# Group attention of a four-layer transformer kernel: first value products in halves, and the contexts and output projections of two blocks joined in one slot each

## Chip, cores and metric

One core of a Trainium2 chip runs the whole program in one launch. The metric is device time in microseconds (us), the median of several executions. All times of instructions come from one profiled execution.

## What is computed

The reference is a residual stack of four parts over x of shape (4, 1024, 256): a windowed attention, a mixture of experts, a second attention over groups, and an expert layer with sinkhorn gates. The change touches only the second attention. Cut to what matters:

```python
Q = x @ wq + bq;  K = x @ wk + bk;  V = x @ wv + bv      # x: (B, S, E) = (4, 1024, 256)
Q, K, V = (t.reshape(B * H, S, D) for t in (Q, K, V))    # H = 16, D = 16
attn = softmax(einsum('bqd,bkd->bqk', Q, K) / sqrt(D))
ctx = einsum('bqk,bkd->bqd', attn, V).reshape(B, S, E)
out = ctx @ wo + bo + x                                  # then a layer norm
```

The plain reshape makes each "head" a group of 64 consecutive tokens with its 256 columns, read as 1024 rows of 16 numbers. So there are 64 independent attentions of 1024 queries by 1024 keys.

## The kernel before

The phases run one after another, with barriers between them. `group_attention` is the phase of the change. It works in 32 **blocks** of 16 **units**. A block is two groups in two halves of the array (h) for one half of the queries; blocks 2m and 2m+1 are a **pair** and together give the tokens of one output tile pair.

TensorE (PE) walks through numbered steps s. Step s does the plain scores of unit s (L1857, two products of 48x512 into one double PSUM bank), of which VectorE (DVE) takes the row maxima (L1781). 26 steps later (LAG), with `back = s - 26`, it does the transposed scores of the same unit (L1870, two products into a ring of three banks), whose exponentials ScalarE (ACT) takes (L1812). The products L1857 and L1870 of a step use different halves of the array's rows and run side by side. Every two steps `weigh` multiplies four exponential tiles with the values (L1886) and adds into one bank, `b_o`. A block has eight such products, each split into two halves of 256 columns on an even and on the following odd step, except the first (kt = 0): it runs at its full width of 512 columns on the even step, and the odd step has none. It waits for ACT's copy of the last block's sums (`o`, L1818), since both use `b_o`.

Each block then needs four transposes of `o` on PE (`context`, L1894, at back % 16 == 6), a reciprocal and a product on DVE (L1792, L1794). Each pair needs four more transposes (`context_T`, L1901), two copies on ACT (L1824), and for each of its blocks an output projection (`project`, L1911), a sum into x and its statistics on DVE (L1800, L1802).

Scores, contexts and projections share two double banks, the **slots** `b_s`. They are used in turn in the order of `step_uses`: PE may write use n only when DVE has read use n-2 (`slot_of`). Order on every engine is that of the program text, so nothing overtakes. SP and POOL only move data: the maxima of a block become a row of the queries by DMAs (`maxima`, L1737 and L1769), which must land before the block's transposed scores, ten steps later, and SP loads the coming queries, keys and values.

Of the kernel before, what the change touches and what calls it, by code (L numbers as in the profile page):

```python
# [14 lines left out]
P = 128  # L15
# [1619 lines left out]
def group_attention(nc, g, parts, values, qs, ks, v):  # L1635
# [12 lines left out]
    MAX_IN = 16 * 2 * P // BL  # L1648
    SHARE = 5
    RB = UB // 2  # L1650
    STEPS = UNITS + LAG + UB + 14

    def block_of(b):
        return b // 4, b // 2 % 2, b % 2
# [12 lines left out]
    def step_uses(s):  # L1667

        uses = [("scores", s)] if s < UNITS else []
        b, j = (s - LAG) // UB - 1, (s - LAG) % UB  # L1670
        if 0 <= b < BLOCKS and j == 6:
            uses.append(("context", b))
        if 0 <= b < BLOCKS and b % 2:
            uses += [("project", b - 1)] * (j == 11) + [("project", b)] * (j == 13)
        return uses

    def transposed_context(back):

        return back // (2 * UB) - 1 if back > UB and back % (2 * UB) == 8 else None

    uses = [use for s in range(STEPS) for use in step_uses(s)]
    use_place = {use: n for n, use in enumerate(uses)}
# [8 lines left out]
    with phase(nc) as (e, semaphore, begin):  # L1691
# [7 lines left out]
        rsum = [sb(f"rsum{s}", [P, HQ, NG]) for s in range(2)]  # L1699
# [71 lines left out]
        @block.vector  # L1771
        def _(dve):
            dve.wait_ge(nmax_zero, ONE + 2)
            for s in range(STEPS):
                for kind, arg in step_uses(s):
                    use = use_place[kind, arg]
                    slot = b_s[use % 2]
                    dve.wait_ge(use_done, ONE + use + 1)
                    if kind == "scores":
                        at, b = column(arg), arg // UB  # L1780
                        nc.vector.tensor_reduce(nmax[b % 2][:, at:at + 1], slot[:], axis=AX.X, op=ALU.max,  # L1781
                                                negate=True).then_inc(use_read, 1)
                        if arg % UB == UB - 1:
                            if b >= 2:
                                dve.wait_ge(max_in[0][b % 2], ONE + MAX_IN * (b // 2))
                                dve.wait_ge(max_in[1][b % 2], MAX_IN * (b // 2))
                            dve.wait_ge(use_read, ONE + use + 1)
                            nc.vector.transpose(max_rows[b % 2][:].bitcast(F32), nmax[b % 2][:].bitcast(F32)).then_inc(rows_ready, 1)  # L1788
                    elif kind == "context":
                        hf = arg % 2  # L1790
                        src = slot[:, 0:HALF].rearrange("p (q n r) -> p q n r", n=NG, r=BL)
                        nc.vector.reciprocal(rsum[hf][:], src[:, :, :, DH]).then_inc(rsum_ready, 1)  # L1792
                        dve.wait_ge(rsum_ready, ONE + arg + 1)
                        nc.vector.tensor_tensor(ctxn[:, :, HQ * hf:HQ * (hf + 1)].rearrange("p n q d -> p q n d"),  # L1794
                                                src[:, :, :, 0:DH],
                                                rsum[hf][:].unsqueeze(3).broadcast_to([P, HQ, NG, DH]), ALU.mult).then_inc(use_read, 1)
                    elif kind == "project":
                        c, gp, h = block_of(arg)
                        t = 2 * (2 * c + h) + gp
                        nc.vector.tensor_tensor(g.x[:, t, :], slot[:, 0:D], g.x[:, t, :], ALU.add).then_inc(use_read, 1)  # L1800
                        dve.wait_ge(use_read, ONE + use + 1)
                        nc.vector.bn_stats(g.stats[:, t, :], g.x[:, t, :]).then_inc(stats_ready, 1)  # L1802

        @block.scalar
        def _(act):
            def weights(back, n):
                w, k = 2 * back + n, back // 2
                h = 1 - back % 2
                act.wait_ge(sT_done, ONE + w + 1)
                if back % 2 == 0 and n == 0 and k >= SETS:  # L1810
                    act.wait_ge(pv_done, ONE + 2 * (k - SETS + 1))
                nc.scalar.activation(probT[k % SETS][2 * h + n][:], b_t[ring_place["weights", w] % RING][:], ACT.Exp, scale=SCALE).then_inc(exp_ready, 1)  # L1812

            def outputs(b):
                act.wait_ge(pv_done, ONE + 2 * RB * (b + 1))
                if b >= 2:
                    act.wait_ge(use_done, ONE + use_place["context", b - 2] + 1)
                nc.scalar.activation(o[b % 2][:], b_o[:], ACT.Copy).then_inc(o_ready, 1)  # L1818

            def context_copy(m):  # L1820
                act.wait_ge(cT_done, ONE + m + 1)
                for h in range(2):
                    src = b_t[ring_place["contextT", m] % RING][:, 2 * P * h:2 * P * (h + 1)].rearrange("p (n a t) -> p n a t", a=A, t=GT)
                    nc.scalar.activation(ctxT[:, h].rearrange("p a n t -> p n a t"), src, ACT.Copy).then_inc(ctxT_ready, 1)  # L1824

            for back in range(UNITS):
                for n in range(2):
                    weights(back, n)
                if back % UB == 3 and back > UB:
                    outputs(back // UB - 1)  # L1830
                if transposed_context(back) is not None:
                    context_copy(transposed_context(back))
            outputs(BLOCKS - 1)
            context_copy(BLOCKS // 2 - 1)

        @block.tensor
        def _(pe):
            def slot_of(use):
                if use >= 2:
                    pe.wait_ge(use_read, ONE + use - 1)  # L1840
                return b_s[use % 2]
# [31 lines left out]
            def weigh(k, first, width):  # L1873

                b, kt = k // RB, k % RB
                c, gp, hf = block_of(b)
                cols = slice(first, first + width)
                if kt == 0:
                    pe.wait_ge(o_ready, ONE + b)
                    if b % 4 == 0:  # L1880
                        pe.wait_ge(v_in[c % SLOTS], ONE + V_IN * (c // SLOTS + 1))
                pe.wait_ge(exp_ready, ONE + NG * (k + 1))
                for h in range(2):
                    for n in range(2):
                        at = BL * (2 * h + n)
                        last = nc.tensor.matmul(b_o[at:at + BL, cols], v[c % SLOTS][:, h, 2 * gp + n, kt, :],  # L1886
                                                probT[k % SETS][2 * h + n][:, cols], start=(kt == 0), stop=(kt == RB - 1 and first > 0))
                last.then_inc(pv_done, 2 * width // HALF)

            def context(b):  # L1890
                slot = slot_of(use_place["context", b])
                pe.wait_ge(o_ready, ONE + b + 1)
                for q in range(HQ):
                    last = nc.tensor.transpose(slot[:, P * q:P * (q + 1)], o[b % 2][:, P * q:P * (q + 1)], g.ident[:])  # L1894
                last.then_inc(use_done, 1)

            def context_T(m):
                bank = ring_bank(ring_place["contextT", m])
                pe.wait_ge(use_read, ONE + use_place["context", 2 * m + 1] + 1)
# [4 lines left out]
            def project(b):  # L1904
                slot = slot_of(use_place["project", b])
                pe.wait_ge(ctxT_ready, ONE + 2 * (b // 2 + 1))
                if b == 0:
                    pe.wait_ge(w_in, ONE + 16 * QT)
                h = b % 2
                for a in range(A):  # L1910
                    last = nc.tensor.matmul(slot[:, 0:D], ctxT[:, h, a].rearrange("p n t -> p (n t)"), wo[:, a, :],  # L1911
                                            start=(a == 0), stop=(a == A - 1))
                last.then_inc(use_done, 1)

            other = {"context": context, "project": project}
            for s in range(STEPS):
# [511 lines left out]
```

## Time and profile before

| | us |
|---|---|
| median of 3 runs | 2508.06 (2502.19 to 2509.59) |
| span of the profiled execution, first to last instruction | 2483.5 |
| `group_attention` in it, first to last reduction of scores | 1395.6 to 2125.1 |
| last work of the phase | about 2171 |
| PE busy in the whole span | 2036.4 (82%) |
| DVE busy | 1642.5 (66%) |
| ACT busy | 1113.8 (45%) |

The time of the profiled execution is known here only as its span; the median of the runs is 24.6 us above it, the start and end outside the instructions included. Busy shares are means over phases of different kinds. What this change is worth is read in the 730 us of its own phase.

### The profile page before, as it was taken

To read this page: it belongs to the slowest core of one execution; us is meant where nothing else is said; L and a number is where in the kernel's file an instruction comes from. 1 tells how busy PE (TensorE), PEld (TensorE's weight loads), DVE (VectorE), ACT (ScalarE), POOL (GpSimd) and SP (SyncE) were. 2 spreads that over 40 slices of the span, in tenths; PEclk is the share of its full clock that TensorE was granted. 3 is DMA by queue.
4 is the path that set the end of the run, shared out by engine and by line. 5 is a ranking of instruction groups with operands and counts; after the bars stand their busy time and mean duration, and the time that the engine had idled before them with its cause. 6 is when DMAs were issued, how large, how long until landed. Compare 5 with 4: busy or idle time off the path is not lost. (4 is left out here: it accounts for less than half of the span.)

```text
span 2483.5 us, 50891 instructions
## 1 busy us (share of the span) xinstructions
PE 2036.4 (82%) x18151; PEld 1397.1 (56%) x18152; DVE 1642.5 (66%) x2882; ACT 1113.8 (45%) x2169; POOL 452.4 (18%) x608
## 2 busy tenths in 40 slices
PE   2888888769889999969968899999999999825052
PEld 2766667448789999958857433333333333324042
DVE  4666666556645555536644679999999989376853
ACT  1555554333233333322223167777777877711000
POOL 2000000010011111113434111111111111030036
PEclk9999999789999999989989779999999999955566
DMA  2000000182131111123349888745744800031036
GB/s 85 2 0 0 0 0 0 70 332 73 42 113 46 49 49 46 46 98 102 104 133 281 166 66 69 48 44 48 52 45 44 69 2 2 1 98 42 0 104 201
DMA packets 207044, 172.12 MB, mean 69 GB/s; under 512 B 121740, under 2 KB 184808, under 8 KB 204744
## 3 DMA queue, kind: packets, MB, share of 16 engines
q1 hardware_dynamic: 186872, 127.44, 27.3%
q0 software_dynamic: 17744, 26.26, 3.9%
q10 hardware_dynamic: 2304, 16.78, 1.8%
q8 instruction: 77, 1.26, 0.3%
q14 instruction: 47, 0.39, 0.1%
HBM read 106.30 MB, written 63.84 MB: 69 GB/s over the span
## 5 line engine op out<-in xcount | busy, mean ns | idle before, releaser
L1781 DVE TENSOR_REDUCE ga_nmax<-banks 128x1 fp32r<-128x1024 f32 x512 | 621.0, 1220 | 55.7 <-PE banks L1857 53.8
L1812 ACT ACTIVATE ga_probT<-banks 128x512 f32<-128x512 f32 x1024 | 553.5, 598 | 189.1 <-PE banks L1870 144.1
L1857 PE MATMUL banks<-a_ks,a_qs 48*128 48x512 f32 x1024 | 382.9, 462 | 28.4 <-DVE ga_nmax L1781 23.1
L1870 PE MATMUL banks<-a_qs,a_ks 49*128 49x512 f32 x1024 | 379.8, 452 | 0.7 <-ACT ga_probT L1812 0.7
L1886 PE MATMUL banks<-ga_probT,a_v 128*32 128x256 f32 (+1 forms) x3840 | 324.8, 411 | 6.3 <-ACT ga_o L1818 6.3
L1857 PEld LDWEIGHTS banks<-a_ks,a_qs 48*128 48x128 f32 x1024 | 161.2, 195 | 242.4 <-DVE ga_nmax L1781 171.0
L1301 PEld LDWEIGHTS banks<-rb_xT,rb_own_w 128*128 128x128 f32 x2272 | 268.0, 194 | 9.4 <-issue 4.9
L1301 PE MATMUL banks<-rb_xT,rb_own_w 128*128 128x128 f32 x2272 | 268.7, 277 | 5.3 <-DMA rb_w<-in_L_ffn_rw_dram 4.7
L1769 POOL DMA_DIRECT2D a_qs<-ga_max_rows x256 | 131.1, 520 | 608.5 <-DVE ga_max_rows L1788 565.3
L1088 PE MATMUL banks<-sh_xnT,sh_w 128*128 128x512 f32 x768 | 183.7, 397 | 27.1 <-DVE sh_w L874 26.0
L1276 ACT ACTIVATE rb_silu<-banks,rb_own_b 128x128 f32<-128x128 f32 x284 | 81.1, 368 | 255.1 <-PE banks L1301 255.1
L1088 PEld LDWEIGHTS banks<-sh_xnT,sh_w 128*128 128x128 f32 x768 | 145.3, 192 | 60.0 <-issue 30.0
L1886 PEld LDWEIGHTS banks<-ga_probT,a_v 128*32 128x32 f32 x3840 | 76.4, 108 | 181.5 <-ACT ga_probT L1812 119.0
L1870 PEld LDWEIGHTS banks<-a_qs,a_ks 49*128 49x128 f32 x1024 | 156.3, 188 | 24.9 <-ACT ga_probT L1812 21.9
L1193 POOL DMA_INDIRECT rb_xb<-normalised_rows,m_source x71 | 67.5, 950 | 475.1 <-PE banks L1295 319.5
L346 DVE TENSOR_REDUCE wa_nmax<-banks 128x4 f32<-128x512 f32 x128 | 86.9, 679 | 100.3 <-PE banks L543 100.3
L1226 DVE SCALAR_TENSOR_TENSOR rb_gluT<-banks,rb_own_b,rb_silu 128x128 f32<-128x128 f32 x284 | 79.9, 344 | 92.0 <-PE banks L1301 92.0
L414 ACT ACTIVATE wa_probT<-banks 128x512 f32<-128x512 f32 x128 | 76.5, 598 | 133.8 <-PE banks L555 133.8
L1323 PE MATMUL banks<-rb_w,rb_gluT 128*128 x568 | 134.5, 380 | 1.4 <-DVE rb_gluT L1226 1.4
L1323 PEld LDWEIGHTS banks<-rb_w,rb_gluT 128*128 128x128 f32 x568 | 102.4, 190 | 12.6 <-issue 1.6
L555 PE MATMUL banks<-ident,wa_prob 128*128 128x128 f32 x512 | 87.2, 295 | 25.1 <-ACT wa_prob L407 25.1
L407 ACT ACTIVATE wa_prob<-wa_ex 128x512 f32<-128x512 f32 x128 | 80.5, 629 | 50.5 <-DVE wa_ex L348 49.7
(288 smaller groups left out, 3055.5 us busy)
## 6 DMA issues: line engine op xcount, KB each, us to landing
sh_xnT<-xnT_parts ACTq DMA_DIRECT2D x16, 1024.0 KB, 5.0
sorted_out<-rb_yb SPq DMA_DIRECT2D x71, 128.0 KB, 1.7
xnT_parts<-np_parts SPq DMA_DIRECT2D x8, 1024.0 KB, 7.7
m_w<-in_L_ffn_rw_dram SPq DMA_DIRECT2D x2, 4096.0 KB, 21.4
values<-pg_v SPq DMA_DIRECT2D x16, 512.0 KB, 3.1
a_v<-values SPq DMA_DIRECT2D x16, 512.0 KB, 8.9
a_qs<-queries_rounded SPq DMA_DIRECT2D x28, 256.0 KB, 8.7
a_ks<-keys_rounded SPq DMA_DIRECT2D x28, 256.0 KB, 10.1
```

Source lines behind the costliest of these rows:

```text
L346: nc.vector.tensor_reduce(nmax[k][:], sc, axis=AX.X, op=ALU.max, negate=True).then_inc(max_ready, 1)
L555: last = nc.tensor.transpose(b_pt[k][:, P * j:P * (j + 1)], prob[k][:, j, :], g.ident[:])
L1088: last = nc.tensor.matmul(bank[m % 2][:], w[a][:, k, P * m:P * (m + 1)], xnT[s][:, b, k, :], start=(k == 0 and a + b == 0), stop=(k == KD ...
L1276: last = nc.scalar.activation(silu[:, m, :], b_p1[:, P * m:P * (m + 1)], ACT.Silu, bias=own_b[s][:, 0, m:m + 1])
L1301: last = nc.tensor.matmul(bank[:, P * m:P * (m + 1)], w[:, k, P * m:P * (m + 1)], xT[s][:, k, :], start=(k == 0), stop=(k == KD - 1))
L1323: last = nc.tensor.matmul(b_y[:, 0:D], gluT[:, m, :], flat[:, bass.ds(n * KH + m, 1), :].rearrange("p o d -> p (o d)"), start=(m == 0), st ...
L1769: nc.gpsimd.dma_start(dst, src).then_inc(max_in[1][b % 2], 16)
L1781: nc.vector.tensor_reduce(nmax[b % 2][:, at:at + 1], slot[:], axis=AX.X, op=ALU.max, negate=True).then_inc(use_read, 1)
L1812: nc.scalar.activation(probT[k % SETS][2 * h + n][:], b_t[ring_place["weights", w] % RING][:], ACT.Exp, scale=SCALE).then_inc(exp_ready, 1)
L1857: return nc.tensor.matmul(slot[:, HALF * kh:HALF * (kh + 1)], qs[a][rows, n, P * q:P * (q + 1)], ks[a][rows, n, HALF * kh:HALF * (kh + 1)] ...
L1870: nc.tensor.matmul(bank[:], ks[a][rows, 2 * gp + n, P * kt:P * (kt + 1)], qs[a][rows, 2 * gp + n, HALF * hf:HALF * (hf + 1)], start=True, ...
L1886: last = nc.tensor.matmul(b_o[at:at + BL, cols], v[c % SLOTS][:, h, 2 * gp + n, kt, :], probT[k % SETS][2 * h + n][:, cols], start=(kt == ...
```

## The change

The first value product of a block runs in two halves like the others. PSUM's start flag is then set on the first half alone, and the second half writes without it. The contexts of both blocks of a pair are transposed together, eight transposes into one slot, at step 7 of the pair's 32 (`CONTEXT_AT`), and DVE takes them with one reciprocal and one product. The pair's `context_T` moves from step 8 to step 13 (`TURN_AT`). Both projections go into one slot at step 18 (`PROJECT_AT`) in place of steps 11 and 13, with one sum and two statistics on DVE. The end of the phase is given six steps more, which hold only the last pair's projection.

```diff
-    STEPS = UNITS + LAG + UB + 14
+    CONTEXT_AT, TURN_AT, PROJECT_AT = 7, 13, 18
+    STEPS = UNITS + LAG + UB + 20
...
-        b, j = (s - LAG) // UB - 1, (s - LAG) % UB
-        if 0 <= b < BLOCKS and j == 6:
-            uses.append(("context", b))
-        if 0 <= b < BLOCKS and b % 2:
-            uses += [("project", b - 1)] * (j == 11) + [("project", b)] * (j == 13)
+        pair, at = (s - LAG) // (2 * UB) - 1, (s - LAG) % (2 * UB)
+        if 0 <= pair < BLOCKS // 2:
+            uses += [("context", pair)] * (at == CONTEXT_AT) + [("project", pair)] * (at == PROJECT_AT)
...
-        return back // (2 * UB) - 1 if back > UB and back % (2 * UB) == 8 else None
+        return back // (2 * UB) - 1 if back > UB and back % (2 * UB) == TURN_AT else None
...
+                        src = slot[:].rearrange("p (q n r) -> p q n r", n=NG, r=BL)
+                        nc.vector.reciprocal(rsum[:], src[:, :, :, DH]).then_inc(rsum_ready, 1)
...
+                        both = g.x[:, t:t + 3:2, :]
+                        nc.vector.tensor_tensor(both, slot[:].rearrange("p (h n) -> p h n", h=2)[:, :, 0:D], both, ALU.add).then_inc(use_read, 1)
                         dve.wait_ge(use_read, ONE + use + 1)
-                        nc.vector.bn_stats(g.stats[:, t, :], g.x[:, t, :]).then_inc(stats_ready, 1)
+                        for h in range(2):
+                            nc.vector.bn_stats(g.stats[:, t + 2 * h, :], g.x[:, t + 2 * h, :]).then_inc(stats_ready, 1)
...
-                                                probT[k % SETS][2 * h + n][:, cols], start=(kt == 0), stop=(kt == RB - 1 and first > 0))
-                last.then_inc(pv_done, 2 * width // HALF)
+                                                probT[k % SETS][2 * h + n][:, cols], start=(kt == 0 and first == 0),
+                                                stop=(kt == RB - 1 and first > 0), skip_group_check=True)
+                last.then_inc(pv_done, 1)
...
-                    k = back // 2 - 2
-                    if k % RB > 0:
-                        weigh(k, HALF // 2 * (back % 2), HALF // 2)
-                    elif back % 2 == 0:
-                        weigh(k, 0, HALF)
+                    weigh(back // 2 - 2, back % 2)
```

On PE, at the change from one block to the next, the program before had these rows from step 4 of the block to the context of step 6. L1886 is the value product, L1857 and L1870 the two kinds of scores, L1894 the context's transposes.

```order
L1886 MATMUL banks<-ga_probT,a_v 32x512 x4
L1857 MATMUL banks<-a_ks,a_qs 128x512
L1870 MATMUL banks<-a_qs,a_ks 128x512
L1857 MATMUL banks<-a_ks,a_qs 128x512
L1870 MATMUL banks<-a_qs,a_ks 128x512
L1857 MATMUL banks<-a_ks,a_qs 128x512
L1870 MATMUL banks<-a_qs,a_ks 128x512
L1857 MATMUL banks<-a_ks,a_qs 128x512
L1870 MATMUL banks<-a_qs,a_ks 128x512
L1886 MATMUL banks<-ga_probT,a_v 32x256 x4
L1894 MATMUL banks<-ident,ga_o 128x128 x4
```

The changed program has these at the end of step 6 and in step 7 of a pair's second boundary (scores are L1856 and L1869 there, the context L1897).

```order
L1886 MATMUL banks<-ga_probT,a_v 32x256 x4
L1856 MATMUL banks<-a_ks,a_qs 128x512
L1869 MATMUL banks<-a_qs,a_ks 128x512
L1856 MATMUL banks<-a_ks,a_qs 128x512
L1869 MATMUL banks<-a_qs,a_ks 128x512
L1886 MATMUL banks<-ga_probT,a_v 32x256 x4
L1897 MATMUL banks<-ident,ga_o 128x128 x8
```

So the pattern of a step (two pairs of scores, one half product) now never breaks, and the context follows one step later with eight transposes instead of four.

On DVE the program before had, over one pair, from the transpose of the maxima (L1788) on, the reductions L1781, the contexts L1792 and L1794, and the projections' sums and statistics L1800 and L1802:

```order
L1788 STREAM_TRANSPOSE ga_max_rows<-ga_nmax 128x32
L1781 TENSOR_REDUCE ga_nmax<-banks 128x1
L1792 RECIPROCAL ga_rsum<-banks 128x16
L1794 TENSOR_TENSOR ga_ctxn<-banks,ga_rsum 128x4x4x16
L1781 TENSOR_REDUCE ga_nmax<-banks 128x1 x5
L1800 TENSOR_TENSOR x<-banks,x 128x256
L1802 BN_STATS stats<-x 128x6
L1781 TENSOR_REDUCE ga_nmax<-banks 128x1 x2
L1800 TENSOR_TENSOR x<-banks,x 128x256
L1802 BN_STATS stats<-x 128x6
L1781 TENSOR_REDUCE ga_nmax<-banks 128x1 x8
```

The changed program has, over the same stretch and up to the next transpose of maxima:

```order
L1787 STREAM_TRANSPOSE ga_max_rows<-ga_nmax 128x32
L1780 TENSOR_REDUCE ga_nmax<-banks 128x1 x2
L1790 RECIPROCAL ga_rsum<-banks 128x32
L1792 TENSOR_TENSOR ga_ctxn<-banks,ga_rsum 128x8x4x16
L1780 TENSOR_REDUCE ga_nmax<-banks 128x1 x11
L1798 TENSOR_TENSOR x<-banks,x 128x2x256
L1801 BN_STATS stats<-x 128x6 x2
L1780 TENSOR_REDUCE ga_nmax<-banks 128x1 x3
```

One context and one projection of twice the size stand where two contexts and two projections stood, and the context has two reductions behind the transpose of the maxima instead of one.

## Rows read from the trace of the kernel before

**Rows 1.** The page's first line and the costliest group of the program.

```profile
span 2483.5 us, 50891 instructions
...
L1781 DVE TENSOR_REDUCE ga_nmax<-banks 128x1 fp32r<-128x1024 f32 x512 | 621.0, 1220 | 55.7 <-PE banks L1857 53.8
```

**Rows 2.** Busy us of PE, PEld, DVE, ACT, POOL, and granted clock, of the phase.

```profile
1468.00:2171.00 703.00, 673.90 (x5924) 268.10 (x5924) 610.73 (x621) 549.02 (x1041) 122.27 (x239) 1.00 0.48 40
```

**Rows 3.** Timeline (start us, length us) of an ordinary step, PE and DVE.

```profile
1799.53 0.49 PE L1857 MATMUL banks<-a_ks,a_qs 48*128 48x512 f32 x1
...
1800.19 0.64 PE L1886 MATMUL banks<-ga_probT,a_v 128*32 128x256 f32 x8
1800.76 0.49 PE L1857 MATMUL banks<-a_ks,a_qs 48*128 48x512 f32 x1
...
1799.07 6.14 DVE L1781 TENSOR_REDUCE ga_nmax<-banks 128x1 fp32r<-128x1024 f32 x5
```

**Rows 4.** Timeline of PE over one block boundary, steps 4 to 7.

```profile
1803.22 0.49 PE L1857 MATMUL banks<-a_ks,a_qs 48*128 48x512 f32 x1
...
1804.15 1.07 PE L1886 MATMUL banks<-ga_probT,a_v 128*32 128x512 f32 x8 [0.20 <-ACT ga_o L1818]
1805.15 0.49 PE L1857 MATMUL banks<-a_ks,a_qs 48*128 48x512 f32 x1
...
1807.33 0.66 PE L1894 MATMUL banks<-ident,ga_o 128*128 128x128 f32 x4
1808.64 0.49 PE L1857 MATMUL banks<-a_ks,a_qs 48*128 48x512 f32 x1 [0.66 <-DVE ga_nmax L1781]
```

**Rows 5.** Timeline of DVE over the same boundary.

```profile
1807.27 0.21 DVE L1788 STREAM_TRANSPOSE ga_max_rows<-ga_nmax 128x32 f32<-128x32 f32 x1
1807.41 1.18 DVE L1781 TENSOR_REDUCE ga_nmax<-banks 128x1 fp32r<-128x1024 f32 x1
1808.51 0.25 DVE L1792 RECIPROCAL ga_rsum<-banks 128x16 f32<-128x16 f32 x1
1808.79 0.42 DVE L1794 TENSOR_TENSOR ga_ctxn<-banks,ga_rsum 128x256 f32<-128x256 f32 x1
1809.41 2.46 DVE L1781 TENSOR_REDUCE ga_nmax<-banks 128x1 fp32r<-128x1024 f32 x2 [0.20 <-PE banks L1857]
```

**Rows 6.** Waits from 1460 to 2180 us: total us, times, longest.

```profile
PE banks L1857 <- DVE ga_nmax L1781: 19.2, 29, 0.9
```

**Rows 7.** Timeline of PE around the pair's transposes and one projection.

```profile
1811.11 0.66 PE L1901 MATMUL banks<-ident,ga_ctxn 128*128 128x128 f32 x4
1811.69 0.49 PE L1857 MATMUL banks<-a_ks,a_qs 48*128 48x512 f32 x1
...
1815.39 1.13 PE L1911 MATMUL banks<-ga_wo,ga_ctxT 128*128 128x256 f32 x4
1816.45 0.50 PE L1857 MATMUL banks<-a_ks,a_qs 48*128 48x512 f32 x1
```

**Rows 8.** Timeline of DVE at that projection.

```profile
1816.55 0.42 DVE L1800 TENSOR_TENSOR x<-banks,x 128x256 f32<-128x256 f32 x1 [0.41 <-PE banks L1911]
1817.01 0.43 DVE L1802 BATCH_NORM_STATS2 stats<-x 128x6 f32<-128x256 f32 x1
1817.36 2.34 DVE L1781 TENSOR_REDUCE ga_nmax<-banks 128x1 fp32r<-128x1024 f32 x2
```

**Rows 9.** An earlier phase's DVE product of twice that size from PSUM (min/median/max ns).

```profile
L1546 DVE TENSOR_TENSOR pg_v<-banks,pg_bv x16: 690/691/692, 1284.2 to 1389.0; 128x512 f32<-128x512 f32 x16
```

**Rows 10.** Timeline of PE, one step at half clock, near the phase's start.

```profile
1445.05 0.79 PE L1857 MATMUL banks<-a_ks,a_qs 48*128 48x512 f32 x1
...
1447.21 0.79 PE L1857 MATMUL banks<-a_ks,a_qs 48*128 48x512 f32 x1
```

**Rows 11.** Timeline of SP's issues of one block's maxima.

```profile
1831.65 4.88 SPq L1737 DMA_DIRECT2D a_qs<-ga_max_rows  x8
```

**Rows 12.** Timeline of the phase's end: the last two projections.

```profile
2167.16 3.04 PE L1911 MATMUL banks<-ga_wo,ga_ctxT 128*128 128x256 f32 x8 [0.84 <-ACT ga_ctxT L1824]
```

More of the change, by code:

```diff
@@ L1698, in group_attention @@
         max_rows = [sb(f"max_rows{s}", [P, BL], F32R) for s in range(2)]
-        rsum = [sb(f"rsum{s}", [P, HQ, NG]) for s in range(2)]
+        rsum = sb("rsum", [P, QT, NG])
         ctxn = sb("ctxn", [P, NG, QT, DH])
@@ L1789, in _ @@
                     elif kind == "context":
-                        hf = arg % 2
-                        src = slot[:, 0:HALF].rearrange("p (q n r) -> p q n r", n=NG, r=BL)
-                        nc.vector.reciprocal(rsum[hf][:], src[:, :, :, DH]).then_inc(rsum_ready, 1)
+                        src = slot[:].rearrange("p (q n r) -> p q n r", n=NG, r=BL)
+                        nc.vector.reciprocal(rsum[:], src[:, :, :, DH]).then_inc(rsum_ready, 1)
                         dve.wait_ge(rsum_ready, ONE + arg + 1)
-                        nc.vector.tensor_tensor(ctxn[:, :, HQ * hf:HQ * (hf + 1)].rearrange("p n q d -> p q n d"),
-                                                src[:, :, :, 0:DH],
-                                                rsum[hf][:].unsqueeze(3).broadcast_to([P, HQ, NG, DH]), ALU.mult).then_inc(use_read, 1)
+                        nc.vector.tensor_tensor(ctxn[:].rearrange("p n q d -> p q n d"), src[:, :, :, 0:DH],
+                                                rsum[:].unsqueeze(3).broadcast_to([P, QT, NG, DH]), ALU.mult).then_inc(use_read, 1)
                     elif kind == "project":
-                        c, gp, h = block_of(arg)
-                        t = 2 * (2 * c + h) + gp
-                        nc.vector.tensor_tensor(g.x[:, t, :], slot[:, 0:D], g.x[:, t, :], ALU.add).then_inc(use_read, 1)
+                        c, gp, _ = block_of(2 * arg)
+                        t = 4 * c + gp
+                        both = g.x[:, t:t + 3:2, :]
+                        nc.vector.tensor_tensor(both, slot[:].rearrange("p (h n) -> p h n", h=2)[:, :, 0:D], both, ALU.add).then_inc(use_read, 1)
                         dve.wait_ge(use_read, ONE + use + 1)
-                        nc.vector.bn_stats(g.stats[:, t, :], g.x[:, t, :]).then_inc(stats_ready, 1)
+                        for h in range(2):
+                            nc.vector.bn_stats(g.stats[:, t + 2 * h, :], g.x[:, t + 2 * h, :]).then_inc(stats_ready, 1)
         @block.scalar
@@ L1816, in outputs @@
                 if b >= 2:
-                    act.wait_ge(use_done, ONE + use_place["context", b - 2] + 1)
+                    act.wait_ge(use_done, ONE + use_place["context", b // 2 - 1] + 1)
                 nc.scalar.activation(o[b % 2][:], b_o[:], ACT.Copy).then_inc(o_ready, 1)
@@ L1871, in scores_T, with weigh @@
                                  qs[a][rows, 2 * gp + n, HALF * hf:HALF * (hf + 1)], start=True, stop=True).then_inc(sT_done, 1)
-            def weigh(k, first, width):
+            def weigh(k, half):
                 b, kt = k // RB, k % RB
                 c, gp, hf = block_of(b)
-                cols = slice(first, first + width)
-                if kt == 0:
+                first = HALF // 2 * half
+                cols = slice(first, first + HALF // 2)
+                if kt == 0 and half == 0:
                     pe.wait_ge(o_ready, ONE + b)
@@ L1886, in weigh, with context @@
                         last = nc.tensor.matmul(b_o[at:at + BL, cols], v[c % SLOTS][:, h, 2 * gp + n, kt, :],
-                                                probT[k % SETS][2 * h + n][:, cols], start=(kt == 0), stop=(kt == RB - 1 and first > 0))
-                last.then_inc(pv_done, 2 * width // HALF)
[L1890 to L1894, printed above, removed]
+                                                probT[k % SETS][2 * h + n][:, cols], start=(kt == 0 and first == 0),
+                                                stop=(kt == RB - 1 and first > 0), skip_group_check=True)
+                last.then_inc(pv_done, 1)
+            def context(m):
+                slot = slot_of(use_place["context", m])
+                pe.wait_ge(o_ready, ONE + 2 * m + 2)
+                for hf in range(2):
+                    for q in range(HQ):
+                        at = HALF * hf + P * q
+                        last = nc.tensor.transpose(slot[:, at:at + P], o[hf][:, P * q:P * (q + 1)], g.ident[:])
                 last.then_inc(use_done, 1)
@@ L1898, in context_T @@
                 bank = ring_bank(ring_place["contextT", m])
-                pe.wait_ge(use_read, ONE + use_place["context", 2 * m + 1] + 1)
+                pe.wait_ge(use_read, ONE + use_place["context", m] + 1)
                 for n in range(NG):
@@ L1902, in context_T, with project @@
                 last.then_inc(cT_done, 1)
[L1904 to L1907, printed above, removed]
+            def project(m):
+                slot = slot_of(use_place["project", m])
+                pe.wait_ge(ctxT_ready, ONE + 2 * (m + 1))
+                if m == 0:
                     pe.wait_ge(w_in, ONE + 16 * QT)
[L1909 to L1912, printed above, removed]
+                for h in range(2):
+                    for a in range(A):
+                        last = nc.tensor.matmul(slot[:, HALF * h:HALF * h + D], ctxT[:, h, a].rearrange("p n t -> p (n t)"), wo[:, a, :],
+                                                start=(a == 0), stop=(a == A - 1))
                 last.then_inc(use_done, 1)
```

## Prediction

> **What bounds the kernel now.** I read the page first for the span and the costliest groups, then the busy time of the phase by engine, then the timeline of PE and DVE over ordinary steps and over one block boundary, and last the list of waits.
>
> The page puts the reductions of scores on DVE on top, 621 us [rows 1], which would make DVE the suspect. The timeline says otherwise. In an ordinary step the first scores start at 1799.53 and again at 1800.76: a step is 1.23 us. DVE's five reductions in 6.14 us are 1.23 each too [rows 3]. Only one of the two sets this pace. A reduction that stands behind other work on DVE takes 1.18 [rows 5], so DVE could be quicker; PE's rows follow each other without a wait. PE is the bound, and in the phase it is busy 673.9 of 703 us at granted clock 1.00 (the 2.4 GHz level), against 610.7 for DVE and 549.0 for ACT [rows 2]. Anything that takes time from PE, or a wait from PE, counts; work on DVE counts only when PE must wait for a slot. The slack for that: DVE ends a reduction at 1799.07 + 1.23 = 1800.30, and PE begins the scores that need its slot at 1800.76 [rows 3]. So DVE may be late by 0.46 us for nothing.
>
> The block boundary is where time is lost. Steps 4, 5 and 6 with the context go from 1803.22 to 1808.64, which is 5.42 us [rows 4]. Three ordinary steps are 3.69. The rest is:
> - the wait for ACT's copy of `o` at step 4: the value product would start 0.66 after the step's start, as in an ordinary step (1800.19 - 1799.53, [rows 3]), and starts 0.93 after it (1804.15 - 1803.22, [rows 4]): 0.27;
> - steps 4 to 6 with the full-width product: up to 1807.33 they take 4.11 [rows 4], of which 3.69 and 0.27 are explained; 0.15 is left. The full product takes 1.00 in place of two halves of 0.57 [rows 3, 4], so PE's own work is 0.14 less, but the scores of step 5 and 6 then come bunched, and PE meets the ring before ACT has emptied it;
> - the context: 1.31 from 1807.33 to 1808.64, of which four transposes are 0.58 (1811.69 - 1811.11 for four of the same size, [rows 7]) and 0.73 is waiting for DVE. The slot that the next scores need is that of step 6, whose reduction could start only behind that of step 5 (late by the bunching) and the transpose of the maxima, at 1807.41, and ended at 1808.59 [rows 5].
>
> PE waits so 29 times, 19.2 us in all [rows 6]: once for each boundary that still has scores behind it.
>
> **The change part by part.**
>
> *Halves.* Steps 4, 5 and 6 become ordinary steps, but for the wait on `o`, which stays: 3 x 1.23 + 0.27 = 3.96 in place of 4.11. Scores are ready for DVE 0.77 after their step's start (step 7: 1808.64 to 1809.41, [rows 4, 5]). So it gets those of step 5 at 1803.22 + 1.23 + 0.27 + 0.77 = 1805.49 and not at 1805.15 + 0.77 = 1805.92. With a reduction of 1.18, 0.27 for the transpose of the maxima (1807.41 - 1805.92 - 1.22, [rows 5]) and another 1.18 it is through with step 6 at 1808.12, and with step 7 at 1809.30.
>
> Here a rule speaks against the change. The rows show 1.14 us for two halves against 1.00 for one full product [rows 3, 4]. The Trainium skill, TensorEngine Tiling, Tiling Modes, says that a change of tiling mode drains TensorE; the halves add one change into the 128x32 tiles and one back per block. The trace agrees as far as it goes, since more than the columns' time is paid twice. By that rule alone the halves would cost 32 x 0.14 = 4.5 us.
>
> By the rows the sum for the three steps comes out the other way, because the wait that the bunching caused (0.15 + 0.14) goes with it. Both effects are in 3.96.
>
> *Contexts joined, at step 7.* Eight transposes are 2 x 0.57, 1.14 us, once per pair. Working on from above in one pair: PE ends step 7 at 1803.22 + 4 x 1.23 + 0.27 = 1808.41, when step 6's slot has been free for 0.29; the transposes end at 1809.55, when step 7's is free too. So step 8's scores wait for nothing. DVE begins the context at 1809.65 and needs 0.30 for the reciprocal (0.25 for half the elements, [rows 5]; twice that at most) and 0.69 for the product ([rows 9], the same number of elements from PSUM; twice 0.42 at most), to 1810.64; step 8's scores are there at 1810.32. DVE is 0.32 late, inside the slack of 0.46. The wait of 0.73 goes at both boundaries.
>
> *`context_T`* moves from step 8 to 13 and costs PE its 0.58 as before. DVE has long written its input and the projection reads it five steps later, so nothing waits.
>
> *Projections joined, at step 18.* PE's work is the same, 2 x 1.06 [rows 7], but in one piece. DVE runs dry in it, and then has one sum of 0.73 to the next start (0.46 for half, to 1817.01, [rows 8], plus the 0.27 that twice the elements add, [rows 8, 9]), and two statistics of 0.35 each (1817.36 - 1817.01, [rows 8]). Counted from the projection's start: PE ends at 2.12, its last row at 2.2; DVE is free at 2.2 + 0.73 + 0.70 = 3.65; step 19's scores are ready at 2.12 + 0.77 = 2.89. DVE is 0.76 late, 0.30 more than the slack. Each step gives back 0.05 (1.23 less 1.18). The scores of step 21 are the first to need step 19's slot, and the wait for `o` at step 20 holds PE for 0.27 anyway. So 0 to 0.30 remain per pair, and the transpose of the maxima at step 21 adds a little. I take 0.2, since the two waits lie one step apart and may not cover each other, for 14 pairs: 2.8 us lost. The bounds are 0 and 0.76, 0 to 10.6 us.
>
> *Waits added.* The context now needs both copies of `o`; the second is the one it needed before, one step longer done. ACT's copy of `o` two blocks on needs the context read; it comes at step 19 and the context is at step 7. SP and POOL get no new wait. Their maxima are issued within 4.88 us of the transpose [rows 11], and ten steps of 1.23 pass before PE needs them.
>
> *The end.* The last pair's context is now one chain: four more transposes (0.57), reciprocal 0.05, product 0.27, sum 0.27, and one more statistic 0.35 behind the eight projection products, which take 3.04 there as before [rows 12]: 1.5 us added. The transposes of block 30, which this takes out of the middle, are in the sum below.
>
> *Sum.* Before: 29 boundaries of 5.42 and the last two, with no scores behind them, of 4.11 + 0.58: 157.2 + 9.4 = 166.6. After: 31 of 3.96 and 15 joined contexts of 1.14: 122.8 + 17.1 = 139.9. Saved 26.7, less 2.8 and 1.5: 22.4 us. Against the profiled execution 2483.5 - 22.4 = 2461.1 for the span; the median lies 24.6 above the span, so **2508.1 - 22.4 = 2485.7**.
>
> **The rivals.** A measurement of this kernel can tell a change from none at about 0.3%, 7.5 us.
>
> 1. *DVE's lateness costs in full.* If the slack is not there when it is needed (the transpose of the maxima and the context come close together), the joined projection costs 0.76 and the joined context 0.32 per pair, 14 x 1.08 = 15.1 in place of 2.8. Saved 26.7 - 15.1 - 1.5 = 10.1: 2498. For it: the slack is read in ordinary steps and the lateness of 0.32 is close to it. Against it: a single projection makes DVE 0.14 late (1817.36 against scores ready at 1816.45 + 0.77, [rows 7, 8]), and PE's 29 waits for a slot are all used up by the contexts [rows 6]. Chance 0.14, of it a third within 0.3%.
>
> 2. *Nothing to measure.* The boundary wait is not removed but moves: for instance PE now meets ACT at the ring, because ACT's copy of `o` stands between exponentials. Against it: ACT has 154 of 703 us free [rows 2], and an ordinary step after the change is the one it keeps up with now. It would have to return 0.6 of the 0.86 saved per boundary (26.7 / 31). Result about 2503. Chance 0.06.
>
> 3. *Slower: PE's clock.* At the half level (1.2 GHz) a step takes 2.16 us [rows 10] and not 1.23, so a stretch at it loses 0.43 of its length. 52 us more of it in this phase cancel the gain; 75 us make 2518. The place would be the joined context, eight transposes in a row. Against it: the clock was 1.00 from 1468 to 2171 [rows 2] with 29 groups of four transposes each followed by a wait of 0.66 [rows 4, 6], and the change takes those waits out. The Trainium skill, TensorE: Matmul & The Clock Gate, PE-mode transpose, says that transposes do not count as work for the clock as matmuls do; by that rule the eight would be 1.1 us of idleness to the gate and the clock might fall. The trace shows no such fall behind four transposes and their wait, together 1.31 us [rows 4]. Chance 0.04.
>
> **How the numbers follow.** My forecast has 0.76: its own range is 2477 to 2493, from the projection's bounds (0 to 10.6 us lost) and some 4 us of spread of a median, whose runs lie 7 us apart. Rival 1 has 0.14, rival 2 0.06, rival 3 0.04. The range that leaves out no more than 2 in 10 reaches from 2477 into rival 1: 2477 to 2500. Faster by over 0.3%: 0.76 + 0.09 = 0.85; within: 0.05 + 0.06 = 0.11; slower: 0.04.
>
> **What the profile after would show.** Halves right: no product of 512 columns at L1886, PE's boundary steps 1.5, 1.23, 1.23. Contexts right: eight transposes in about 1.2 us and the waits of PE for DVE down from 29 of 0.66 to near none; if there are 14 of 0.3 or more at step 9, rival 1. Projections right: eight products in 2.1 us, a DVE gap of about 1.6 before the sum, then a PE wait at step 21 of at most 0.3. A pair would take 44.0 us in place of 45.6. Wrong altogether would be a granted clock below 1.00 between 1470 and 2150, or a new wait of PE for ACT at L1870.

## The result, and the profile after

The changed kernel took 2472.38 us in the median (2458.29 to 2486.32, 4 runs) against 2505.12 (2496.21 to 2509.59, 4 runs) of the kernel before: ratio 0.9865, 95% interval 0.983 to 0.9899. It is faster by 33 us, where 22.4 were forecast, and lies below the range.

The page's first line of the traced execution, which took 2472.21 us:

```profile
span 2470.5 us, 51323 instructions
```

So a run's time is 1.7 us above its span. The 24.6 us between span and median, which were taken to include the start and end outside the instructions, were something else: the traced execution of the kernel before was quicker than the timed ones. Its part behind the attention phase took 312.4 us (2171.1 to 2483.5), where the same part took 339.9 in this trace (2130.6 to 2470.5). The experiments show where such a difference comes from (E1, and *The base* below). The two spans can't be compared. The phase itself can, since in both traces it spends about as long at the half clock (62 us from its start to the rise of the clock). It went from 775.5 us (1395.6 to 2171.1) to 747.0 (1383.6 to 2130.6), 28.5 less.

PE over a pair's second boundary in the changed kernel, from the timeline (start us, length us); the rows answer to [rows 4]:

```profile
1819.36 0.49 PE L1856 MATMUL banks<-a_ks,a_qs 48*128 48x512 f32 x1
...
1820.30 0.64 PE L1886 MATMUL banks<-ga_probT,a_v 128*32 128x256 f32 x8 [0.20 <-ACT ga_o L1817]
1820.86 0.49 PE L1856 MATMUL banks<-a_ks,a_qs 48*128 48x512 f32 x1
...
1822.10 0.50 PE L1856 MATMUL banks<-a_ks,a_qs 48*128 48x512 f32 x1
...
1823.33 0.49 PE L1856 MATMUL banks<-a_ks,a_qs 48*128 48x512 f32 x1
...
1824.56 1.09 PE L1897 MATMUL banks<-ident,ga_o 128*128 128x128 f32 x8
1825.58 0.50 PE L1856 MATMUL banks<-a_ks,a_qs 48*128 48x512 f32 x1
```

Step 4 takes 1.50 (1819.36 to 1820.86), steps 5 and 6 1.24 and 1.23, as forecast. The eight transposes take 1.02, not 1.14, and the scores behind them start without a wait. Of PE's waits for results of other engines from 1460 us to the end of the phase (total us, times, longest; [rows 6] before) none is for DVE's reductions any more. This one is left at every boundary:

```profile
PE banks L1886 <- ACT ga_o L1817: 6.2, 30, 0.2
```

DVE at the same context and at the pair's projection, to be read against [rows 5] and [rows 8]:

```profile
1825.69 0.36 DVE L1790 RECIPROCAL ga_rsum<-banks 128x32 f32<-128x32 f32 x1 [0.25 <-PE banks L1897]
1826.08 0.69 DVE L1792 TENSOR_TENSOR ga_ctxn<-banks,ga_rsum 128x512 f32<-128x512 f32 x1
1826.69 7.05 DVE L1780 TENSOR_REDUCE ga_nmax<-banks 128x1 fp32r<-128x1024 f32 x6
...
1841.75 0.69 DVE L1798 TENSOR_TENSOR x<-banks,x 128x512 f32<-128x512 f32 x1 [1.27 <-PE banks L1914]
1842.47 0.75 DVE L1801 BATCH_NORM_STATS2 stats<-x 128x6 f32<-128x256 f32 x2
1843.14 3.47 DVE L1780 TENSOR_REDUCE ga_nmax<-banks 128x1 fp32r<-128x1024 f32 x3
```

Behind the context DVE's next reduction starts at 1826.69, when its scores have been ready since 1825.58 + 0.77 = 1826.35: 0.34 late, where 0.32 was forecast. And PE at that projection, against [rows 7]:

```profile
1839.71 1.99 PE L1914 MATMUL banks<-ga_wo,ga_ctxT 128*128 128x256 f32 x8
1841.64 0.50 PE L1856 MATMUL banks<-a_ks,a_qs 48*128 48x512 f32 x1
...
1842.87 0.49 PE L1856 MATMUL banks<-a_ks,a_qs 48*128 48x512 f32 x1
...
1843.81 0.64 PE L1886 MATMUL banks<-ga_probT,a_v 128*32 128x256 f32 x8 [0.21 <-ACT ga_o L1817]
1844.41 0.50 PE L1856 MATMUL banks<-a_ks,a_qs 48*128 48x512 f32 x1
```

The projection takes 1.93 in one piece, not 2 x 1.06. DVE's next reduction starts at 1843.14, when its scores have been ready since 1841.64 + 0.77 = 1842.41: 0.73 late, 0.76 forecast. PE pays 0.03 for it, and the rest is hidden behind the wait for the copy of `o` (1843.81 to 1844.41 is 0.60, where an ordinary half product takes 0.57). Busy time over 614 us of the full-clock part (the stretch's columns are those of [rows 2]), before and then after:

```profile
1468.00:2082.00 614.00, 590.48 (x5232) 233.81 (x5232) 564.44 (x566) 483.91 (x917) 110.58 (x217) 1.00 0.55 46
```

```profile
1468.00:2082.00 614.00, 608.03 (x5702) 243.29 (x5700) 574.64 (x551) 509.21 (x961) 114.36 (x224) 1.00 0.53 45
```

PE went from 96% to 99% busy, at granted clock 1.00 in both.

### The profile page after: what moved, and what is told of

The parts are those of the page before. It is cut to its first block and busy times, and to the rows that moved or that the text cites. A ratio compares the mean times of both kernels' runs of the same rounds, so it can differ in the third digit from the quotient of the medians.

```text
span 2470.5 us, 51323 instructions
## 1 busy us (share of the span) xinstructions
PE 2022.8 (82%) x18407; PEld 1392.6 (56%) x18408; DVE 1626.6 (66%) x2834; ACT 1117.2 (45%) x2169; POOL 451.7 (18%) x608
## 5 line engine op out<-in xcount | busy, mean ns | idle before, releaser
L1780 DVE TENSOR_REDUCE ga_nmax<-banks 128x1 fp32r<-128x1024 f32 x512 | 610.4, 1218 | 32.7 <-PE banks L1856 31.6
L1856 PE MATMUL banks<-a_ks,a_qs 48*128 48x512 f32 x1024 | 390.9, 465 | 9.2 <-PEq L77 5.3
L1869 PE MATMUL banks<-a_qs,a_ks 49*128 49x512 f32 x1024 | 380.3, 451 | 0.0
L1886 PE MATMUL banks<-ga_probT,a_v 128*32 128x256 f32 x4096 | 331.6, 397 | 6.4 <-ACT ga_o L1817 6.4
L1856 PEld LDWEIGHTS banks<-a_ks,a_qs 48*128 48x128 f32 x1024 | 158.8, 194 | 224.5 <-DVE ga_nmax L1780 171.6
L1886 PEld LDWEIGHTS banks<-ga_probT,a_v 128*32 128x32 f32 x4096 | 81.4, 108 | 197.6 <-ACT ga_probT L1811 152.5
L1869 PEld LDWEIGHTS banks<-a_qs,a_ks 49*128 49x128 f32 x1024 | 154.1, 188 | 10.1 <-ACT ga_probT L1811 8.8
```

Of the source, the lines that this page charges most:

```text
L1856: return nc.tensor.matmul(slot[:, HALF * kh:HALF * (kh + 1)], qs[a][rows, n, P * q:P * (q + 1)], ks[a][rows, n, HALF * kh:HALF * (kh + 1)] ...
```

## Experiments

All are compared with the kernel before in the same set of runs. Besides the ratio I read from each trace the time of one pair at the full clock, between transposes of the maxima two blocks apart. It does not depend on the phase's start at the half clock or on the other phases, and repeats within 0.02 us from pair to pair and from trace to trace, except that in some traces a boundary now and then takes 0.1 to 0.3 more. "Saved" is against 45.55.

| kernel | us per pair | saved | ratio (interval) |
|---|---|---|---|
| before | 45.55 | | 1.000 (E1: 0.9971 to 1.0028) |
| halves alone, E3 | 44.71 | 0.84 | 0.9937 (0.9912 to 0.9962) |
| halves in all blocks but the first two, E6 | 44.72 | 0.83 | 0.9942 (0.992 to 0.9964) |
| joined contexts alone, E11 | 44.36 | 1.19 | 0.993 (0.990 to 0.996) |
| both joins alone, E4 | 44.03 | 1.52 | 0.9914 (0.9886 to 0.9941) |
| halves and joined projections, E8 | 44.75 | 0.80 | 0.9941 (0.992 to 0.9962) |
| halves and joined contexts, E9 | 43.67 | 1.88 | 0.9875 (0.9819 to 0.993) |
| the whole change | 43.53 | 2.02 | E2: 0.9849 (0.9823 to 0.9875) |
| the whole, projection at step 25, E10 | 43.78 | 1.77 | 0.9877 (0.9828 to 0.9926) |
| the whole, copy of `o` earlier, E7 | 43.54 | 2.01 | 0.9861 (0.9835 to 0.9887) |

**E1 and E2, both kernels again.** No edit.

> The kernel before, unchanged, timed and traced once more. In the first traces the attention phase took 775.5 us before (1395.6 to 2171.1) and 747.0 after (1383.6 to 2130.6), 28.6 us less, but the part ahead of it was 12.0 shorter after and the part behind it 27.6 longer, 312.4 to 340. Theory A: those two have nothing to do with the change and wander from run to run. Then this trace has the phase at 775 to 776 and the part ahead of it or behind it moved by several us; ratio to the kernel before 0.997 to 1.003. Theory B: the parts outside belong to the kernel; then they come again within 2 us (1395.6 ahead, 312.4 behind).

> The changed kernel, unchanged, with more rounds. Theory A: phase again 747.0 within 0.5 us, the parts outside at other values than 1383.6 and 340, ratio 0.9885 (28.6 of 2505) within the spread. Theory B (the change also shortens the part ahead of the phase): phase start near 1384 again, and a ratio near the 0.9865 measured or below.

E1's traced execution was a long one: span 2528.3, the phase 793.7 us, its start at 1395.3 as before, the part behind it 339.3. E2 had phase 739.5, start 1390.1, behind 336.8. So theory B falls: the part behind the phase is long with both kernels here, and the 27 us were not the change's. In these traces that part goes with the chip. The four kernels run with E1 all had 337 to 342 there, the eight others later on two other chips 312 to 314, and the kernel before took 2506.2 in the median on the first and 2478.4 and 2478.7 on the others. Theory A was half right: the phase wanders too, 793.7 where 775 to 776 was expected, and 739.5 where 747.0 was. The windows of E1 show why (granted clock is the third number from the end):

```profile
1440.00:1500.00 60.00, 60.00 (x330) 20.27 (x324) 34.59 (x31) 29.99 (x56) 6.23 (x13) 0.50 0.56 54
1510.00:1530.00 20.00, 19.79 (x174) 8.19 (x175) 17.82 (x18) 15.49 (x31) 1.82 (x4) 1.00 1.05 65
```

PE is busy without a gap for 60 us and the clock stays at the half level (1.2 GHz), until about 1505. In the first trace of before it rose near 1458, so this stretch is 47 us longer in E1, and the phase 18.2. The part ahead of the phase moves as well: over all 14 traces the phase starts between 1383.6 and 1401.4. From each run's span and mean clock follows its time at the half level, span x (1 - clock) x 2: from 454 to 536 us in the 35 runs of before made with E1 to E4 (2498 to 2530 us). With [rows 10]'s price, 0.43 us per us at that level, the runs come together: time less 0.43 of it is 2298 to 2307 for before, 2269 to 2274 for E2, about 30.5 apart in the mean. This is an estimate, since the price was read in the phase alone. E2's six runs had 457 us at the half level and before 480 on average, which by the same price is another 10 us; the means of the two lie 40.6 apart, the medians 38.

**E3 and E4, the halves and the joins apart.**

```diff
-                    if k % RB > 0:
-                        weigh(k, HALF // 2 * (back % 2), HALF // 2)
-                    elif back % 2 == 0:
-                        weigh(k, 0, HALF)
+                    weigh(back // 2 - 2, back % 2)
```

E3 makes this edit in the kernel before; E4 takes it back in the changed one.

> The kernel before with nothing but the first value product in halves. Theory A (PE bound, DVE's slack is used up at the boundary): steps 4 to 6 take 3.96 in place of 4.11, and PE's wait for a slot behind each context falls from 0.66 to about 0.4, since the reduction of step 5 starts 0.43 earlier; 0.47 per boundary, 29 x 0.47 + 2 x 0.15 = 14 us, phase 761.5. Rival: the halves cost PE 0.14 each and the wait stays, phase 775 to 780.

> The changed kernel with the first value product back at full width, so the two joins alone. Theory A: each boundary has the bunched 4.11 again (+0.15, 31 times), and DVE, late by the bunching, makes PE wait some 0.3 at the joined context (15 times): phase 747 + 9 = 756. Rival (the joins do all of it, the halves nothing): 747. Sum of E3 and E4 against the whole: 14 + 19.5 = 33.5 against 28.6, so the parts overlap by some 5 us: both remove the same wait of PE for DVE.

PE in E3 at the context, from the timeline:

```profile
1785.88 0.50 PE L1857 MATMUL banks<-a_ks,a_qs 48*128 48x512 f32 x1
...
1787.11 0.66 PE L1896 MATMUL banks<-ident,ga_o 128*128 128x128 f32 x4
1788.14 0.50 PE L1857 MATMUL banks<-a_ks,a_qs 48*128 48x512 f32 x1 [0.38 <-DVE ga_nmax L1781]
```

The wait of 0.66 is 0.38 with the halves, at 25 boundaries between 1516 and 2080 us. A pair saves 0.84, forecast 0.94 (2 x 0.47). In E4 the bunched steps are back, 1788.90 to 1793.01, the 4.11 of [rows 4], and the pair is 0.50 longer than the whole change's. PE from step 7 on in E4:

```profile
1793.01 0.50 PE L1856 MATMUL banks<-a_ks,a_qs 48*128 48x512 f32 x1
...
1794.33 1.09 PE L1895 MATMUL banks<-ident,ga_o 128*128 128x128 f32 x8
1795.46 0.50 PE L1856 MATMUL banks<-a_ks,a_qs 48*128 48x512 f32 x1
```

Step 7 takes 2.45, where the whole change has 2.25 (1823.33 to 1825.58): of the 0.3 of waiting for DVE that was expected at the joined context, 0.2 shows. The phases, 756.3 in E3 and 751.6 in E4, are 5 us shorter than forecast, but they hold a shorter stretch at the half clock than the first traces and are no measure. Halves and joins sum to 2.36 and give 2.02 together. The working for this: both remove the same wait for DVE. Of its 2 x 0.66 per pair the halves alone leave 2 x 0.38 and the joins alone 0.2, so about 0.36 is counted in both.

**E5 and E6, is the clock's gain from the halves?** In the kernel before:

```diff
-                    if k % RB > 0:
+                    if k % RB > 0 or k // RB < 2:
```

E6 has `>= 2` in place of `< 2`; both with the start flag on the first half alone.

> The kernel before with halves in its first two blocks only, those that start while TensorE's clock is at the half level. So far, by span x (1 - mean clock) x 2 of each run, the time at the half level is 480 us on average in 35 runs of the kernel before, 479 in 11 of the joins alone, and 465, 457 and 468 in 7, 6 and 4 runs of kernels with halves; 25 of the first 46 are long ones over 475, against 3 of 17. Theory C: the halves at the phase's start let the clock rise earlier. Then this run has some 462 us at the half level and is 6 to 9 us faster than before, ratio 0.997, of which only 0.3 us come from the two boundaries themselves. Rival: chance, or the later blocks; then half-level time 480 and ratio 1.000.

> The kernel before with halves in all blocks but the first two. Theory C: time at the half level as before, 480 us on average with long ones among them; 0.86 us saved for each warm pair, some 12 us: ratio 0.9952, and E3 (0.9937) the better by E5's share. Rival (the clock gains come from the halves later on, or from chance): half-level time near 462 and a ratio as E3's.

E5: ratio 1.0004 (0.998 to 1.0029), 454 us at the half level on average in 12 runs, against 456 in 29 of before. E6: 0.9942 (0.992 to 0.9964), 457 us. On this chip the halves at the phase's start change nothing that can be measured, and all of the halves' gain is in the later boundaries. But this is another chip than that of E1 to E4, and the kernel before had no long stretches to shorten here: 456 us and not 480. (In the expectation of E5 the count of long runs should read 24 of the first 46 and 2 of 17.) So theory C got no support, and its case, a chip where before has 480, was not tried again.

**E7, the copy of `o` earlier**, to take the last wait at a boundary away. In the changed kernel:

```diff
+                if back % UB == 3 and back > UB:
+                    outputs(back // UB - 1)
                 for n in range(2):
                     weights(back, n)
-                if back % UB == 3 and back > UB:
-                    outputs(back // UB - 1)
...
+                if 4 <= back <= UNITS + 3 and back % UB == 3:
+                    weigh(back // 2 - 2, 1)
                 if s < UNITS:
...
-                if 4 <= back <= UNITS + 3:
+                if 4 <= back <= UNITS + 3 and back % UB != 3:
                     weigh(back // 2 - 2, back % 2)
```

> The changed kernel with the last half product of a block moved ahead of the scores of its step 3, and ACT's copy of the sums ahead of that step's exponentials. Theory A says that PE's wait of 0.27 for the copy at step 4 is all that is left at a boundary besides its own work: it goes, 31 x 0.27 = 8 us, a pair takes 43.0 in place of 43.53, ratio 0.9815 to before. Rival: the copy now delays two exponentials by 0.5, the ring of three banks makes PE wait for them at step 3 or 4, and the wait only moves: pair 43.5, ratio 0.985.

The rival held: the wait for the copy is gone, and the pair is as long as in the changed kernel. Steps 3 to 5 in its timeline, PE and then ACT:

```profile
1754.08 0.64 PE L1886 MATMUL banks<-ga_probT,a_v 128*32 128x256 f32 x8
1754.64 0.49 PE L1856 MATMUL banks<-a_ks,a_qs 48*128 48x512 f32 x1
...
1755.92 0.49 PE L1869 MATMUL banks<-a_qs,a_ks 49*128 49x512 f32 x1
1756.34 0.64 PE L1886 MATMUL banks<-ga_probT,a_v 128*32 128x256 f32 x8
1756.91 0.49 PE L1856 MATMUL banks<-a_ks,a_qs 48*128 48x512 f32 x1
...
1754.78 0.60 ACT L1817 ACTIVATE ga_o<-banks 128x512 f32<-128x512 f32 x1 [2.24 <-PE banks L1886]
1755.28 13.10 ACT L1811 ACTIVATE ga_probT<-banks 128x512 f32<-128x512 f32 x22
```

From 1754.08 to 1756.91 are steps 3 and 4, 2.83 us, where the changed kernel takes 2.77 for them (1798.11 to 1800.88) with the wait for the copy. The last transposed scores of step 4, at 1755.92, come late. They need a bank of the ring whose exponential could start only behind the copy, at 1755.28, and each takes 0.60: PE waits for ACT there instead.

**E8 to E11, which join gives what.** E8 has a context per block again at step 6, E9 and E11 a projection per block again, at steps 18 and 20 of the pair and not at 11 and 13 as in the kernel before; E11 also has the full first product.

```diff
-            uses += [("context", pair)] * (at == CONTEXT_AT) + [("project", pair)] * (at == PROJECT_AT)
+            uses += [("context", pair)] * (at == CONTEXT_AT)
+            uses += [("project", 2 * pair)] * (at == PROJECT_AT) + [("project", 2 * pair + 1)] * (at == PROJECT_AT + 2)
```

(E9 and E11; in E8 the projections are joined and the contexts as in the kernel before.) E10 has `PROJECT_AT` 25.

> The changed kernel with its contexts apart again, one per block at step 6 with four transposes, halves and joined projection kept. Theory A: the wait of PE for the slot of step 6 is back at both boundaries, 0.4 each, as in E3; DVE has two reciprocals and products to do: a pair takes 43.53 + 2 x 0.4 + 0.1 = 44.4. If the joined projection were what matters, the pair would stay near 43.6.

> The changed kernel with its projections apart again, at steps 18 and 20, halves and joined contexts kept. By E8 against E3 (44.76 and 44.71 us per pair) joining the projections gives nothing beside halves and single contexts: PE's eight products are 1.93 in place of 2 x 1.06, and DVE's lateness of 0.73 takes it back at the next context. In this kernel no wait follows, so the 0.19 of PE should show: a pair takes 43.53 + 0.2 = 43.7, the phase 3 us more than the changed kernel's, ratio to it within what can be measured. Rival: the joined projection is worth as much as my sum was short, 0.4 per pair: 43.95.

> The changed kernel with the joined projection at step 25, far from a block boundary, so that no wait for ACT's copy of the sums lies behind it. My working has DVE 0.76 late behind it (0.73 in the trace) and a slack of 0.46: PE should wait some 0.25 to 0.3 for the slot at step 28, 14 times, a pair 43.53 + 0.28 = 43.8. If the slack is larger than that, 43.5.

> The kernel before with nothing but the joined contexts (step 7, turn at 13, single projections at 18 and 20, first product at full width). Joins alone took 44.02 per pair; by E8 and E3 the projections add 0 to 0.2 to that, so 44.0 to 44.2, and the joined contexts alone save 1.4 to 1.5 of the 2.04 of the whole change. If the joins need each other, it is nearer 44.7.

E8: 44.75, longer than my 44.4. At the pair's first boundary DVE is still late from the joined projection when the single context comes, and PE waits 0.60 there, with 0.38 again at the second:

```profile
1772.91 0.65 PE L1900 MATMUL banks<-ident,ga_o 128*128 128x128 f32 x4
1774.16 0.50 PE L1861 MATMUL banks<-a_ks,a_qs 48*128 48x512 f32 x1 [0.60 <-DVE ga_nmax L1783]
```

That takes back the 0.19 that joining the projections saves on PE. With joined contexts no such wait follows: E9 is 0.14 longer than the whole change. E10, the projection away from the boundary, is 0.25 longer, mainly by a wait of PE for the slot that the changed kernel lacks, at step 28:

```profile
1765.05 1.99 PE L1914 MATMUL banks<-ga_wo,ga_ctxT 128*128 128x256 f32 x8
...
1769.73 0.50 PE L1856 MATMUL banks<-a_ks,a_qs 48*128 48x512 f32 x1 [0.23 <-DVE ga_nmax L1780]
```

Forecast were 0.25 to 0.3. So the slack of 0.46 fits, and at step 18 it is the wait for `o` that covers what goes beyond it. E11 saves 1.19 per pair; I had expected 1.4 to 1.5. I had put the projections' share too low: without the halves they add 0.33. Joining them and moving one of them off step 20, which is a bunched step in E11, are not told apart by this.

**E12, the changed kernel on a quicker chip.**

> The changed kernel once more, for its time at the half level beside that of the kernel before on the same chip. On one chip before had 480 us at that level and the kernels with halves 457 to 468; on another it had 456 and kernels with halves in some or all blocks 454, 457, 451 and 457. If the change shortened it, it does so here too (10 us or more, ratio 0.985); if not, the two agree within 5 us, and the ratio is what the phase alone gives, 30 us: 0.988.

2446.74 against 2478.68 in the median, ratio 0.9864 (0.9825 to 0.9903), 32 us. Time at the half level: 452 us in 6 runs against 455 in 16 of before. Here the clock gave about 1 us, and nearly the whole gain is the phase's own.

## Why the prediction was right in its mechanism and wrong in its size

*The bound.* Right. PE paced the phase, and the wait for DVE at the contexts went in full (29 waits of 0.66 on average, and none after).

*Halves.* Right: steps 4 to 6 take 3.97, forecast 3.96, and alone they save 0.84 per pair. On the rule of the Trainium skill, TensorEngine Tiling, Tiling Modes (a change of tiling mode drains TensorE): the rows show a price, as halves cost 1.14 where the full product cost 1.00, though no run shows that it is the drain. E3 shows the other side larger.

*Contexts joined.* Right in mechanism. The eight transposes were mis-sized: 1.02, not 1.14, so 0.12 per pair. One group of four costs 0.57 and four more in the same piece add 0.45. My reading is that the second four have no change of kind of work in front of them; no run isolates this.

*Projections joined.* This term was the most wrong. I took PE's work as unchanged and 0.2 lost per pair to DVE's lateness. PE's work fell by 0.19 (2.12 to 1.93), and the lateness, 0.73 measured, cost 0.03. Together 0.36 per pair. (The terms of the lateness, 2.2 + 0.73 + 0.70 less 2.89, add up to 0.74 and not to 0.76.)

*The sum.* These make 0.48 per pair, 7 us for 14.5 pairs: 22.4 + 7 = 29.4, against 28.5 measured in the first two traces, whose stretches at the half clock are equally long, and 30.5 from the runs of E2 at equal half-level time. The step that failed is thus the working of the two joined pieces. For PE's work I took twice the single price (1.14 and 2.12, measured 1.02 and 1.93), and for the projection I took 2.8 us lost to DVE's lateness, where the trace has 0.03 a pair, 0.4 us.

*The range.* Its own bounds, 0 to 10.6 us lost and 4 us of spread, give 2479 to 2497 around a base of 2508.1; the 2477 and 2493 given for the forecast don't follow from them. The median fell 13.3 us below the forecast: 7 by the mis-sized terms, 3 because a fourth run took the median of the kernel before from 2508.1 to 2505.1, and some 3 that the phase's working doesn't hold.

*What is left of 33 to 38 us.* On the chip of E1 to E4, up to 8 us more came with a shorter time at the half level, 457 to 468 us in the runs with halves (E2, E3 and the first ones) and 479 to 480 in those without (before and E4). On the two others no such difference is clear: 454, 457, 451 and 457 us in E5 to E8 against 456, and 449, 444, 452 and 452 in E9 to E12 against 455. Whether the change acts on the clock on one chip, or few runs happened to fall so, is not settled; E5 and E6 did not run on the first chip.

*Rivals.* Rival 1, lateness in full, did not happen, and E10 shows where a part of it would. Rival 2 did not happen to this change but is just what E7 met. Rival 3 did not: the clock was 1.00 with eight transposes in a row. That speaks against a worry one could take from the Trainium skill, TensorE: Matmul & The Clock Gate, PE-mode transpose, for a group of this length between dense products.

*The base.* Taking the saving off the median was sound. Taking the gap between span and median for an offset was not, though the forecast of the median does not use it. The gap was most likely one between chips. The traced execution's part behind the phase, 312.4 us, is that of E5 to E12. Its time less 0.43 of its 472 us at the half level is 2282, inside the 2280 to 2288 of the kernel before on those two chips and outside the 2298 to 2307 on that of E1 to E4. The first four timed runs of the changed kernel give 2268 to 2273 this way, as E2 does. The chips of the first runs are not on record.

## What to carry to other kernels

When one engine paces a loop, another may be late by a slack that the timeline shows (from the end of a read to the next write into the same slot), and a larger piece is best put just ahead of a wait that exists anyway. A joined piece on the pacing engine can cost less than twice the single one (1.02 against 1.14, 1.93 against 2.12), while an engine that was covered before may become late behind it. Such changes are compared by the loop's period at full clock, and not by the spans of two executions, which for one and the same kernel lay 45 us apart here (2483.5 and 2528.3, probably on two chips).

## What was not expected of the hardware

The clock stayed at the half level for 60 us and more of gapless PE work in E1, and in the first trace of the same program it rose 47 us earlier. The part behind the attention phase took 337 to 342 us on one chip and 312 to 314 on others. In the last phase of the first trace of before the DMA moved about 205 GB/s, in that of after about 150:

```profile
GB/s 2 2 2 1 2 0 2 54 354 40 0 53 68 89 53 52 105 0 0 0 0 0 0 0 1 0 0 2 2 263 129 218 199 209 231 204 205 205 30 0
```

```profile
GB/s 2 0 0 76 353 21 0 61 91 58 52 52 105 0 1 0 0 0 0 0 0 0 0 4 1 262 151 179 183 167 126 154 169 132 118 106 144 0 0 0
```

These are the transfers' rates in 40 slices from 2100 us to the end, before and then after. The code there is the same in both kernels, and E1, the kernel before on the chip of E2 to E4, has the lower rates too.
